# Feed-forward of a decoder layer: the clamp's difference moved from VectorE to GpSimd, the residual sum from GpSimd to VectorE

## The reference, cut to what matters

```python
def _qdot(x, w, out_dtype=BF16):
    return jnp.dot(x.astype(E4M3), w.astype(E4M3), preferred_element_type=out_dtype)
ff_gate = _qdot(x, w_gating[0])            # 256 -> 1024
gate_value = jax.nn.gelu(ff_gate)
ff1 = _qdot(x, w_gating[1])                # 256 -> 1024
activations = gate_value * ff1
outputs = _qdot(activations, w_linear)     # 1024 -> 256
...
x = x + _L0_ffn_ref(_layernorm(x, axis=-1), ...)
```

## Time and profile before

| | |
|---|---|
| median of 3 runs | 1701.81 us (1698.41 to 1705.91) |
| profiled execution, own time | 1701.85 us |
| its span in the trace | 1699.0 us |
| busy over the span | PE 1529.6 us (90%), DVE 1405.3 us (83%), ACT 1123.5 us (66%), POOL 743.4 us (44%) |
| feed-forward, from about 1594 us to the end | 105 us of the span |
| in it | DVE busy 80.88 us, ACT 64.55 us, PE 56.99 us, POOL 26.00 us |

### The profile page before, as it was taken

How to read it: one execution, slowest core, us unless ns; L and a number is a source line. 1 busy time by engine, 2 the same in 40 slices (tenths; PEclk the granted TensorE clock), 3 DMA queues, 4 the chain that set the end, 5 groups by cost and what they waited for, 6 DMA issues and landing times. The chain is left out here.

```text
span 1699.0 us, 44072 instructions
## 1 busy us (share of the span) xinstructions
PE 1529.6 (90%) x18002; PEld 1291.3 (76%) x18002; DVE 1405.3 (83%) x2505; ACT 1123.5 (66%) x2187; POOL 743.4 (44%) x725
## 2 busy tenths in 40 slices
PE   4989899998639999999999999999999999999456
PEld 4777777776517888888888888888888888888224
DVE  3788888887475889989889889899898898898587
ACT  1666666665336777777777777777777777776474
POOL 0465655565163344444434434534444444343014
PEclk9999999999778999999999999999999999999677
DMA  8000000000032111111111111111111111110001
GB/s 221 1 1 1 1 1 1 2 1 1 26 123 62 40 48 50 51 50 51 43 46 50 50 50 51 41 48 50 50 50 50 39 49 50 51 50 2 1 12 33
DMA packets 43289, 67.91 MB, mean 40 GB/s; under 512 B 9365, under 2 KB 41810, under 8 KB 42962
## 3 DMA queue, kind: packets, MB, share of 16 engines
q1 hardware_dynamic: 43090, 65.11, 13.3%
HBM read 63.26 MB, written 1.84 MB: 38 GB/s over the span
## 5 line engine op out<-in xcount | busy, mean ns | idle before, releaser
L1115 POOL TENSOR_TENSOR xa_CW<-xa_CTX,xa_CH 128x500 fp32r<-128x500 f32 x187 | 306.8, 1641 | 591.5 <-ACT xa_CH L1309 591.5
L1337 DVE TENSOR_TENSOR xl_ACC<-xl_ACC,xl_PB 125x896 f32<-125x896 f32 x320 | 439.1, 1372 | 11.0
L1301 ACT ACTIVATE xl_PB<-banks,xl_BIB,xl_SCB 125x896 f32<-125x896 f32 x384 | 401.3, 1096 | 31.5 <-PE banks L1173 31.5
L1328 DVE TENSOR_SCALAR xl_PB<-xl_PB 125x896 f32<-125x896 f32 x384 | 248.8, 648 | 64.6 <-ACT xl_PB L1301 63.5
L1283 ACT ACTIVATE xl_V<-banks 125x256 f32<-125x256 f32 x384 | 147.9, 385 | 154.8 <-PE banks L1140 154.8
L1140 PE MATMUL banks<-xa_WVhigh,xa_CH 128*125 128x256 f32 x768 | 238.5, 311 | 0.0
L1140 PE MATMUL banks<-xa_WVlow,xa_CH 128*125 128x256 f32 x768 | 215.8, 281 | 0.0
L1140 PE MATMUL banks<-xa_WVhigh,xa_CW 128*125 128x256 f32 x768 | 215.7, 281 | 0.0
L1274 ACT ACTIVATE xl_KXhigh<-banks,xa_bk 128x500 fp32r<-128x500 f32 x192 | 130.5, 680 | 100.1 <-PE banks L1140 100.1
L1189 PE MATMUL banks<-xl_PB,xl_V 125*32 125x112 f32 x6144 | 187.2, 262 | 1.5 <-DVE xl_PB L1328 1.5
L1344 DVE SCALAR_TENSOR_TENSOR xl_KXlow<-banks,xa_bk,xl_KXhigh 128x500 fp32r<-128x500 f32 x192 | 137.4, 716 | 54.9 <-ACT xl_KXhigh L1274 54.1
(11 more groups left out here) (223 smaller groups left out, 3772.9 us busy)
## 6 DMA issues: line engine op xcount, KB each, us to landing
xa_CTX<-in_ctxT SPq DMA_DIRECT2D x93, 500.0 KB, 3.6
fw_QUT<-in_W_quT SPq DMA_DIRECT2D x1, 2048.0 KB, 13.0
fw_WO<-in_W_o SPq DMA_DIRECT2D x1, 2048.0 KB, 18.9
xq_WR<-in_w_gating SPq DMA_DIRECT2D x1, 2048.0 KB, 9.4
X<-in_x SPq DMA_DIRECT2D x1, 1792.0 KB, 9.6
out<-ff_R SPq DMA_DIRECT2D x16, 112.0 KB, 1.9
xa_CTX<-in_ctxT SPq DMA_DIRECT2D x1, 1500.0 KB, 14.8
xq_WL<-in_w_linear SPq DMA_DIRECT2D x1, 1024.0 KB, 11.7
```

What stands on the lines that cost most here:

```text
L1115: nc.gpsimd.tensor_tensor(context_piece(CW, i), context_piece(CTX, i), context_piece(CH, i), ALU.subtract).then_inc(ctx_low, 1)
L1301: nc.scalar.activation(PB[t % PR][:, :, :], banks[0:TK, 2 * i:2 * i + KT, 0:QW], ACT.Exp, scale=SCB[j][:, t:t + 1], bias=BIB[j][:, t:t + 1 ...
L1328: nc.vector.tensor_scalar(pt, pt, E_HI, E_LO, ALU.min, ALU.max).then_inc(clipped, 1)
L1337: nc.vector.tensor_tensor(ACC[j][:, :, :], prev[:, :, :], PB[t % PR][:, :, :], ALU.add).then_inc(summed, 1)
```

## The change

`D8` = `H8` - `C8` is issued by POOL instead of DVE. The residual sum `R` = `X` + `Y` is issued by DVE instead of POOL, in a new helper `add_output`, behind `A8`. `T8` is made one pass later than its product, `A8` three passes after the product instead of two, so that the loop has one pass more (35 instead of 34). `keep_output` stands ahead of `A8` instead of at the end of the pass. Pass n of DVE's loop is now: `C8` of n-2, `PR_` of n, `T8` of n-1, `Y` where there is one, `A8` of n-3, `rows` where there is one, `R` where there was a `Y`.

```diff
             @block.gpsimd
-                for g in range(PAIRS):
-                    it, p = g // PPS, g % PPS
-                    pool.wait_ge(y_ready, g + 1)
-                    if it:
-                        pool.wait_ge(stored[p], it * 16)
-                    nc.gpsimd.tensor_tensor(R[p][:, :], X[:, g, :], Y[g % 2][:, :], ALU.add).then_inc(r_ready, 1)
+                for u in range(FF_UNITS):
+                    pool.wait_ge(clamped, u + 1)
+                    if u >= 2:
+                        pool.wait_ge(a_ready, u - 1)
+                    nc.gpsimd.tensor_tensor(D8[u % 2][:, :], H8[u % 2][:, :], C8[u % 2][:, :], ALU.subtract).then_inc(rest_ready, 1)
             @block.vector
+                def add_output(g):
+                    it, p = g // PPS, g % PPS
+                    dve.wait_ge(y_ready, g + 1)
+                    if it:
+                        dve.wait_ge(stored[p], it * 16)
+                    nc.vector.tensor_tensor(R[p][:, :], X[:, g, :], Y[g % 2][:, :], ALU.add).then_inc(r_ready, 1)
-                for n in range(FF_UNITS + 2):
-                    u = n - 2
-                    if u >= 0:
+                for n in range(FF_UNITS + 3):
+                    if 2 <= n < FF_UNITS + 2:
+                        u = n - 2
                         dve.wait_ge(half_ready, u + 1)
                         nc.vector.tensor_scalar(C8[u % 2][:, :], H8[u % 2][:, :], FP8_MAX / 2, -FP8_MAX / 2, ALU.min, ALU.max).then_inc(clamped, 1)
...
-                        if u >= 0:
-                            dve.wait_ge(half_ready, u + 1)
+                        if n >= 2:
+                            dve.wait_ge(t_ready, n - 1)
                         nc.vector.tensor_tensor(PR_[i][:, :], GV[i][:, :], UP[i][:, :], ALU.mult).then_inc(prod_ready, 1)
-                    if u >= 0:
-                        dve.wait_ge(clamped, u + 1)
-                        nc.vector.tensor_tensor(D8[u % 2][:, :], H8[u % 2][:, :], C8[u % 2][:, :], ALU.subtract).then_inc(rest_ready, 1)
-                    if n < FF_UNITS:
-                        dve.wait_ge(prod_ready, n + 1)
-                        nc.vector.tensor_scalar(T8[n % 4][:, :], PR_[n % 2][:, :], FP8_MAX, -FP8_MAX, ALU.min, ALU.max, saturate=False).then_inc(t_ready, 1)
-                    if u >= 0:
+                    if 1 <= n < FF_UNITS + 1:
+                        u = n - 1
+                        dve.wait_ge(prod_ready, u + 1)
+                        nc.vector.tensor_scalar(T8[u % 4][:, :], PR_[u % 2][:, :], FP8_MAX, -FP8_MAX, ALU.min, ALU.max, saturate=False).then_inc(t_ready, 1)
+                    if n < FF_UNITS and pair_after(n) is not None:
+                        keep_output(pair_after(n))
+                    if n >= 3:
+                        u = n - 3
...
                     if n < FF_UNITS and pair_after(n) is not None:
-                        keep_output(pair_after(n))
+                        add_output(pair_after(n))
                 for g in range(outputs_before(FF_UNITS), PAIRS):
                     keep_output(g)
+                    if g > outputs_before(FF_UNITS):
+                        add_output(g - 1)
+                add_output(PAIRS - 1)
```

## The result

The changed kernel takes 1705.27 us (median of 20 runs, 1701.13 to 1710.40), the kernel before, run beside it, 1701.70 us (20 runs). The ratio is 1.0023, with a 95% interval of 1.0013 to 1.0033. So it is slower by some 3.6 us, less than the 0.5% that the prediction called telling; the forecast was 1703.5 us and no change.

What follows compares the result with a forecast made beforehand. DVE was taken to set the feed-forward's pace, by 0.2 us a pass over ACT. The terms' +1.65 us on the profiled 1701.85 us gave 1703.5 us, no change that can be told, with a range of 1691 to 1711.

Steps and rivals of the forecast that it cites:

- Where the difference is served: Plain passes: the waiting difference gets in only when DVE stops at A8 a pass later; two passes take 4.51 us.
- (a): DVE's passes: differences are served in order of issue, behind PR, and T waits; 1706.6 us, chance 0.17.
- 6 plain passes: Passes without ff_X or ff_Y, set by DVE: 0.26 us more each, +1.6 us.
- 9 passes with ff_X: The waiting difference gets in at ff_X: 2.40 us a pass, 0.10 more each, +0.9 us.
- 8 passes with ff_Y: POOL works under and behind ff_Y, and the sum joins DVE: 2.50 us, 0.19 more each, +1.5 us.
- what the sums on POOL took from DVE: Time DVE lost to sums on POOL goes: 0.62 us three times and 0.35 once, -2.2 us.
- 6 waiting passes: Two passes behind each turn of rows: the difference finds DVE idle and costs 0; without that cover 0.26 us each.
- pass 2: It has no A8 any more; ACT's pace holds it at 1.86 us instead of 2.31: -0.45 us.
- drain: From C of unit 30 to the end of the last A: 4.2 us instead of 3.78, +0.4 us.
- last sum: Behind the drain, on DVE, it ends 1.10 us after the last ff_Y's start: -0.1 us.
- (b): The difference is hidden, POOL working beside PR and T: -10.4, so 1691.5 us, chance 0.12.
- (c): No cover: POOL is served only when DVE stands at A8; +12.3, so 1714.1 us, slower, chance 0.12.

Runs made afterwards that it cites:

- e1: The changed kernel with only the difference D8 put back on DVE behind the product: 1701.63 us, ratio 1.0001 to the kernel before.
- e3: The changed kernel with the difference left out, A8 made from C8 and POOL empty: 1689.44 us, ratio 0.9923 to the kernel before.
- e2: The changed kernel with the residual sum put back on POOL, behind the difference, which stays there: 1707.83 us, ratio 1.0040 to the kernel before.
- e7: The changed kernel with rows made early and one scratch operation of 256 columns, on 112 or 128 partitions, between A8 and C8 in five passes; only its trace is read.
- e9: The changed kernel with rows made early and one scratch operation on 120, 96, 64, 32 or 16 partitions between A8 and C8; only its trace is read.
- e4: The changed kernel with the residual sum between ff_Y and A8 instead of behind A8: 1705.09 us, ratio 1.0019 to the kernel before.
- e10: The changed kernel with rows made early and scratch operations on 112 partitions in other places, two with full-width operations behind them; only its trace is read.
- e5: The kernel before with the rows of all four groups normalized and widened at the start: 1685.50 us, ratio 0.9914 to the kernel before.

## Why the prediction was right, point by point

**That POOL and DVE exclude each other here, so that the change moves work and hides none.** Right, and it decided the case. e1 puts the whole loss on the difference, e3's trace prices it at 14.0 us on POOL and 11.5 on DVE, e2 shows the same for the sum.

**Where the difference is served.** This step failed: "Nothing lets it in until DVE stops at `A8`". I had concluded it from the 10.20 us of the earlier trace rows, in front of which stands an ff_Y on 112 partitions. It holds only behind such an operation. Of the 30 differences that met DVE at work, 15 came in right behind PR, as rival (a) has it, among them those of 4 of the 6 plain passes; 15 were kept out. The price agrees nearly by chance, since the time is exclusive wherever it is taken: 2.23 us where I had 2.24 to 2.25 and (a) 2.17, and 4.62 for the two passes that went as I had described, for which I had 4.51.

**The terms**, forecast and measured from the starts of C, in us:

| | forecast | measured |
|---|---|---|
| 6 plain passes | +1.6 | +1.7 |
| 9 passes with ff_X | +0.9 | +1.3 |
| 8 passes with ff_Y | +1.5 | +3.0 |
| what the sums on POOL took from DVE | -2.2 | -2.2 |
| 6 waiting passes | 0 | -0.2 |
| pass 2 | -0.45 | -0.3 |
| drain | +0.4 | +0.5 |
| last sum | -0.1 | +0.1 |
| together | +1.65 | +3.9 |

A pass with ff_X took 2.43 where I had 2.40, and 2.55 once, where the difference was served behind PR ahead of the first ff_X of a group and so covered nothing. What is left to the span's 4.7 lies outside: +0.3 ahead of the first product, +0.5 behind the last sum; no cause of either was looked for.

**The term that was mis-sized** is the passes with ff_Y. Five took 2.57 us instead of 2.50 (one of them with ff_X's 0.32 on top); A8, held back by POOL, lost 0.46 and not 0.39. The other three took 2.9, as in rival (a), which gave 2.84: the difference was served behind PR, and ff_Y covered nothing. In two of them DVE had just waited for `H8`, by 0.08 us; in the third no operation on 112 partitions had run since DVE's last stop. The first of the three:

```profile
1643.15 1.07 POOL L1594 TENSOR_TENSOR ff_D<-ff_H,ff_C 128x448 bf16<-128x448 fp8e4 x1 [1.92 <-DVE ff_C L1636]
1643.29 1.18 DVE L1647 TENSOR_SCALAR ff_T<-ff_PR 128x448 fp8e4<-128x448 bf16 x1
```

**The sum on DVE**, 0.41 us long and a pitch of 0.33, came as taken. **The waiting passes** came out near what was said of them in sum, not each: the pass behind unit 4 took 2.25 instead of 1.98, since ACT's pace of 1.80 was not what had held it; two that waited for PE got shorter by 0.2.

**The rivals.** (b), hidden, would have been 10 us faster; e3, with nothing on POOL, shows that some 12 us were there to be had, and the changed kernel had none of them. (c), no cover, is refuted by A8's 1.07 and ff_X's 1.07: the difference was served wherever ff_Y or ff_X came by while it was waiting. (a) describes the 15 differences above, not the rest. Its total, 1706.6 us, lies 1.3 above the 1705.27 measured, mine 1.8 below: the time can't tell the two orders of service apart, and that mine came within 2 us owes something to terms that lie close together under both.

## What to carry to other kernels

Before work is moved to GpSimd to run beside VectorE, look in the trace for a GpSimd operation that crosses VectorE's two-input or fast one-input operations on SBUF: if either is stretched, moving gives VectorE's time back with interest (0.79 for 0.54 us here). Count as free only what falls under VectorE's stops or its reads of PSUM (ff_Y covered 0.33 us of the difference's 0.79, ff_X only 0.12), and expect the gain to shrink when the stops are removed. A list of waits pointed to the better change: VectorE's longest wait was for rows that VectorE itself made late, while it stood idle 6.4 us at the start.

## What the runs showed of the hardware

A GpSimd request that finds VectorE in a full queue is served at the next boundary, or not at all, depending on an earlier operation. After a VectorE operation on 16, 32, 64, 96 or 112 partitions it was kept out behind the product, and in most of these cases until VectorE stopped or read PSUM, for up to 10.2 us; after one on 120 or 128 partitions it was served within 0.2 us (one and eight cases; e7 to e9). A full-width operation in between doesn't clear this (e4, e10), a stop does. The changed kernel's trace fits: ff_X, ff_Y and ff_R all have 112 partitions.

A VectorE operation that GpSimd itself holds up clears it as a stop does. In e2 ff_Y stands ahead of an A8 that waits 1.09 us for GpSimd, and the next difference is served behind PR at once:

```profile
1670.85 0.41 DVE L1625 CAST ff_Y<-banks 112x256 bf16<-112x256 f32 x1
1671.19 1.70 DVE L1659 SCALAR_TENSOR_TENSOR ff_A<-ff_D,ff_T 128x448 bf16<-128x448 bf16 x1
1672.81 0.85 DVE L1639 TENSOR_SCALAR ff_C<-ff_H 128x448 bf16<-128x448 fp8e4 x1
1673.58 0.38 DVE L1646 TENSOR_TENSOR ff_PR<-ff_GV,ff_UP 128x448 bf16<-128x448 bf16 x1
1673.88 1.17 DVE L1650 TENSOR_SCALAR ff_T<-ff_PR 128x448 fp8e4<-128x448 bf16 x1
```

The second sum of the earlier trace rows got in right behind the first for the same reason: its C had been held up (0.53). So the rule reads: a request is kept out if, since VectorE last stopped, an operation on 112 partitions or fewer has been issued; and an operation that GpSimd holds up begins the count anew, itself included. I call it a stop when an operation starts over 0.05 us later than its usual distance. In the ten traces in which GpSimd works beside VectorE (both kernels, e2, e4 to e10), 259 requests met VectorE at work, and for 256 of them the rule gives whether the next VectorE operation was stretched. The other three stand in the drain: in two VectorE stopped for 0.12 us right behind the request (the kernel before and e5), in the third its next operation waited for the difference itself (e2). The rule was made from these same traces, so the count shows that it fits, not that it holds elsewhere.

The Trainium skill, "SBUF — State Buffer", section "Who interferes with whom", has the one issued first served first. The passes without a narrow operation (one on 112 partitions or fewer) agree (ff_T waits, 1.17 us), the ones behind a narrow operation don't. The border between 112 and 120 is where the last sixteen partitions begin; "GPSIMD Engine Reference" of the Trainium skill, section "Specifications", gives each of GpSimd's eight cores sixteen partitions, the last one 112 to 127. That a VectorE operation which leaves that core's partitions alone changes how the next requests are served is a guess from this; no run shows the mechanism.
